# A Fourier-layer tower on one core: SBUF-to-SBUF seams, earlier group loads, and another order of squares in the mix

## The reference, cut to what matters

```python
for l in range(LAYERS):                                   # 4
    xf = rfft2(h)                                         # of every image and channel
    top = einsum('bixy,ioxy->boxy', xf[:, :, :16, :16], w1)
    bot = einsum('bixy,ioxy->boxy', xf[:, :, -16:, :16], w2)
    sc = irfft2(top and bot put into zeros)
    pw = einsum('bihw,oi->bohw', h, pw_w[l]) + pw_b[l]
    y = sc + pw
    y = (y - y.mean((0, 2, 3))) * rsqrt(y.var((0, 2, 3)) + EPS)   # over all images
    h = gelu(y * gamma[l] + beta[l])
```

## Time and profile before

| | |
|---|---|
| time before, median of 3 runs | 4336.68 us (4324.19 to 4337.49) |
| time of the profiled execution | 4346.47 us |
| its span, first to last instruction | 4344.7 us |
| mean granted TensorE clock | 0.880 of full speed |
| PE busy | 3227.5 us (74%) |
| DVE busy | 2415.4 us (56%) |
| ACT busy | 2244.2 us (52%) |
| POOL busy | 173.2 us (4%) |
| DMA moved | 798.68 MB, mean 184 GB/s |

### The profile page before, as it was taken

How to read it: one execution, slowest core, us unless ns; L and a number is a source line. 1 busy time by engine, 2 the same in 40 slices (tenths; PEclk the granted TensorE clock), 3 DMA queues, 4 the chain that set the end, 5 groups by cost and what they waited for, 6 DMA issues and landing times. The chain is left out here.

```text
span 4344.7 us, 119303 instructions
## 1 busy us (share of the span) xinstructions
PE 3227.5 (74%) x52804; PEld 1863.9 (43%) x52804; DVE 2415.4 (56%) x2474; ACT 2244.2 (52%) x2644; POOL 173.2 (4%) x249
## 2 busy tenths in 40 slices
PE   6758888885577677757577776755999996659777
PEld 4544444444444344435344343444444442543432
DVE  4545555554477677646577676744333332554556
ACT  3545566654466556546456555644666664222321
POOL 2013100000000000000000000000010102000000
PEclk8879999997799889878899888987999998669688
DMA  8857666667768878787678787887343331002042
GB/s 287 308 150 186 173 155 157 172 188 281 242 181 242 248 218 260 209 282 263 214 220 252 216 239 242 245 290 257 120 163 148 142 121 32 1 19 61 1 102 66
DMA packets 172143, 798.68 MB, mean 184 GB/s; under 512 B 31177, under 2 KB 37649, under 8 KB 122286
## 3 DMA queue, kind: packets, MB, share of 16 engines
q1 hardware_dynamic: 160796, 776.18, 58.8%
q0 software_dynamic: 7936, 13.65, 1.0%
q10 hardware_dynamic: 2898, 1.17, 0.1%
HBM read 448.68 MB, written 342.23 MB: 182 GB/s over the span
## 5 line engine op out<-in xcount | busy, mean ns | idle before, releaser
L828 PEld LDWEIGHTS bank<-fb,arena 64*64 64x64 f32 x16384 | 555.7, 196 | 540.1 <-issue 484.1
L828 PE MATMUL bank<-fb,arena 64*64 64x128 f32 x16384 | 619.7, 289 | 196.5 <-issue 140.7
L1045 ACT ACTIVATE arena<-bank 128x1024 f32<-128x1024 f32 x384 | 383.5, 1023 | 638.7 <-PE bank L973 423.7
L845 DVE TENSOR_TENSOR arena<-bank,arena 128x1024 f32<-128x1024 f32 x384 | 467.2, 1217 | 411.4 <-PE bank L828 408.8
L837 DVE STREAM_TRANSPOSE arena<-bank 128x1024 f32<-128x1024 f32 x256 | 318.8, 1245 | 535.7 <-PE bank L818 535.6
L1088 DVE STREAM_TRANSPOSE arena<-arena 128x1024 f32<-128x1024 f32 x384 | 458.3, 1212 | 134.2 <-ACT arena L1035 132.2
L818 PE MATMUL bank<-arena,ga 64*64 64x256 f32 x4096 | 308.8, 413 | 300.0 <-DMA arena<-spec_out 242.0
L973 PE MATMUL bank<-arena,wst 64*64 64x512 f32 x3072 | 414.7, 620 | 17.1 <-issue 11.1
L1052 ACT ACTIVATE arena<-arena 128x1024 f32<-128x1024 f32 x384 | 403.2, 1050 | 0.3
L1038 ACT ACTIVATE arena<-arena,shift,scale 128x1024 f32<-128x1024 f32 x256 | 316.3, 1236 | 129.2 <-DVE arena L845 127.0
L818 PEld LDWEIGHTS bank<-arena,ga 64*64 64x64 f32 x4096 | 167.3, 142 | 430.9 <-issue 359.3
(11 more groups left out here) (238 smaller groups left out, 3647.1 us busy)
## 6 DMA issues: line engine op xcount, KB each, us to landing
y_dram<-arena SPq DMA_DIRECT2D x384, 512.0 KB, 8.2
arena<-y_dram SPq DMA_DIRECT2D x96, 2048.0 KB
arena<-spec_in SPq DMA_DIRECT2D x32, 2048.0 KB, 10.0
spec_out<-arena SPq DMA_DIRECT2D x128, 512.0 KB, 8.2
arena<-in_w_modes SPq DMA_DIRECT2D x28, 2048.0 KB, 14.2
arena<-spec_out SPq DMA_DIRECT2D x112, 512.0 KB, 10.4
spec_in<-arena SPq DMA_DIRECT2D x96, 512.0 KB, 7.9
spec_in<-arena SPq DMA_DIRECT2D x8, 2048.0 KB, 12.5
```

Source lines behind the costliest of these rows:

```text
L828: mm = pe.matmul(hpx(bank[2 * s + i][CHAN[v], :])[:, :, j * S:(j + 1) * S], a2[p % 2][CHAN[i], :, v, 4 * T + j], hpx(fb2[CHAN[i], :]), sta ...
L845: dve.tensor_tensor(chunk(p, T), slot(s), chunk(p, T), ALU.add).then_inc(y_added, 1)
L1045: act.activation(chunk(p, T), slot(NEXT_SLOT[T]), ACT.Copy).then_inc(evicted, 1)
```

## The change

Of the fuse, three things change. Piece n+1 of the groups is issued at step n, where piece n was. The last group of new spectra goes straight from `xs` to the mix's buffer `s_sb` in four SBUF-to-SBUF copies of 64 KB for chunk 0 and four for chunk 1 (`load_last_group`); the seven earlier groups of these chunks are loaded from HBM ahead of it (`next_spectra`: for chunk 0 before the next layer's weights). The group is still stored to HBM too, for the chunks behind.

Of the seams: the barriers between the stages of the tower are gone, and named semaphores stand in their place. The part of the last mix chunk that pair 0 reads goes from `m_sb` to `grp[0]` in four SBUF-to-SBUF copies, ahead of the chunk's store. The last unit is turned before its sums are taken, and the batch norm's tiny chain is split up and runs between the fuse's first instructions. `m_sb` and `x2` move to other addresses, so that they don't lie on what the end of the fuse still reads.

Of the mix: `mix_done` is signalled for each half of a unit, ACT takes both squares ahead of the copies of the next product, and DVE takes its crosses in the order 0, 1 with no square behind them.

```diff
@@ sync_mix
+                for t in range(4):
+                    row = t % 2 * C + t // 2 * HB
+                    if c == NCH - 1:
+                        sp.dma_start(grp[0]...[row:row + HB, c],
+                                     m_sb[c % 2][t * HB:(t + 1) * HB, 0]...).then_inc(grp_loaded[0], 16)
                 for t in range(4):
                     sp.dma_start(spec_out[c, row:row + HB] ...
...
+                sp.wait_ge(spec_stored, l * (NG * 64) + 64)
+                sp.wait_ge(p_stored[0], l * (USES * 64))
+            load(2)
@@ tensor_mix.spectra
-                mm.then_inc(mix_done, 1)
+                    if swap == 1:
+                        mm.then_inc(mix_done, 1)
@@ scalar_mix
             for n in range(NU):
                 square(n, 0)
+                square(n, 1)
                 if n + 1 < NU:
                     for h in range(2):
                         copy_product(n + 1, h)
-                square(n, 1)
@@ vector_mix
-            for n in range(NU):
-                cross(n, 1)
+            for n in range(NU - 1):
                 cross(n, 0)
+                cross(n, 1)
                 turn(n)
...
+            turn(NU - 1)
+            cross(NU - 1, 1)
+            cross(NU - 1, 0)
@@ sync_fuse
+            def next_spectra(c, b, later):
+                sp.wait_ge(p_stored[b], l * (USES * 64) + USES * 64)
+                sp.wait_ge(squared, (l * NP + NP - later) * 4)
+                sp.wait_ge(spec_stored, l * (NG * 64) + (NG * 64))
+                load_spectra(sp, c, slice(0, NG - 1))
-            load_group(sp, l, 0, slice(NCH - 1, NCH))
+            load_piece(sp, l, 0)
             for n in range(NP + 2):
-                if n < NP:
-                    load_piece(sp, l, n)
+                if n + 1 < NP:
+                    load_piece(sp, l, n + 1)
                 if n > 1 and (n - 2) % Q == Q - 1:
+                    if n == NP + 1:
+                        sp.wait_ge(hdft_turned, (l * NP + NP) * 2)
+                        load_last_group(sp, 0, from_planes)
                     store_spectra((n - 2) // Q)
...
+                if n == NP - 1:
+                    next_spectra(0, 1, 2)
+            next_spectra(1, 3, 0)
+            sp.wait_ge(s_last_group, l * 128 + 192)
+            load_last_group(sp, 1, from_planes)
@@ tensor_fuse and tensor_last
+            pe.wait_ge(mixed_turned, (l * NU + NU - 1) * 2)
             rows_of(0, 0)
+            tensor_sums(pe, l)
             rows_of(0, 1)
@@ vector_fuse and vector_last
             turn_rows(dve, l, 0, 0, ROWS_SLOT[0])
+            vector_variance(dve, l)
             turn_rows(dve, l, 0, 1, ROWS_SLOT[1])
+            vector_scale(dve, l)
@@ each engine's program
-                phase_end(sp, l * 2 + 2)
                 sync_fuse(sp, l, False)
-                phase_end(sp, l * 2 + 3)
```

More of the change, by code:

```diff
@@ L546, in ahead @@
                         load_pair(sp, l, p)
-            for c in range(3):
-                load(c)
+            if first:
+                for c in range(2):
+                    load_spectra(sp, c, slice(0, NG - 1))
+                    if c > 0:
+                        sp.wait_ge(s_last_group, 64)
+                    load_last_group(sp, c, lambda c, v, ro: spec_in[c, ro * C + v * HB:ro * C + v * HB + HB, NG - 1])
+            else:
+                sp.wait_ge(spec_stored, l * (NG * 64) + 64)
+                sp.sem_inc(waited[sp.engine], 1)
+                sp.wait_ge(p_stored[0], l * (USES * 64))
+                sp.sem_inc(waited[sp.engine], 1)
+            load(2)
             for u in range(2):
@@ L632, in rotate @@
                 if c > 1:
-                    act.wait_ge(mix_done, (l * NCH + c) * 2 - 2)
-                act.activation(r_sb[c % 2][0:C], s_sb[c % 3][C:P], ACT.Copy, scale=-1.0).then_inc(imag_up, 1)
+                    act.wait_ge(mix_done, (l * NCH + c) * 4 - 4)
+                else:
+                    if c == 0 and not first:
+                        act.wait_ge(p_stored[2], l * (USES * 64))
+                        act.sem_inc(waited[act.engine], 1)
+                    act.activation(r_sb[c][0:C, 0:NG - 1], s_sb[c][C:P, 0:NG - 1], ACT.Copy, scale=-1.0)
+                    act.wait_ge(s_last_group, l * 128 + c * 64 + 64)
+                    act.sem_inc(waited[act.engine], 1)
+                gs = slice(NG - 1 if c < 2 else 0, NG)
+                act.activation(r_sb[c % 2][0:C, gs], s_sb[c % 3][C:P, gs], ACT.Copy, scale=-1.0).then_inc(imag_up, 1)
             def copy_product(n, h):
@@ L661, in scalar_mix @@
                         copy_product(n + 1, h)
-                square(n, 1)
                 if n % 2 == 0 and n // 2 + 1 < NCH:
                     rotate(n // 2 + 1)
-            act.wait_ge(bn_step, l * BN_STEPS + 7)
-            act.sem_inc(waited[act.engine], 1)
-            act.activation(bn[:, 14:15], bn[:, 13:14], ACT.Sqrt).then_inc(bn_root, 1)
+            scalar_root(act, l)
         BN_STEPS = 12
@@ L706, in turn @@
                     dve.sem_inc(waited[dve.engine], 1)
-                dve.wait_ge(s_squared, (l * NU + n) * 2 + 2)
+                if n == 2 and not first:
+                    dve.wait_ge(spec_stored, l * (NG * 64) + 64)
+                    dve.sem_inc(waited[dve.engine], 1)
+                if n == NU - 1:
+                    dve.wait_ge(mix_done, (l * NU + n) * 2 + 2)
                 dve.sem_inc(waited[dve.engine], 1)
@@ L1002, in h_dft @@
                 mm.then_inc(hdft_done, 1)
+            pe.wait_ge(mixed_turned, (l * NU + NU - 1) * 2)
+            pe.sem_inc(waited[pe.engine], 1)
             rows_of(0, 0)
+            tensor_sums(pe, l)
             rows_of(0, 1)
@@ L1032, in gelu @@
                 n = l * NP + p
+                if p == 0 and T == 0:
+                    act.wait_ge(bn_step, l * BN_STEPS + 12)
+                    act.sem_inc(waited[act.engine], 1)
                 if first:
@@ L1100, in h_turn @@
                 dve.wait_ge(hdft_done, l * NP + p + 1)
+                if p == 0:
+                    dve.wait_ge(mixed_stored[1], l * (NCH * 32) + NCH * 32)
+                    dve.sem_inc(waited[dve.engine], 1)
                 if q == 0:
@@ L1271, in gelu @@
             def gelu(p, T):
+                if p == 0 and T == 0:
+                    act.wait_ge(bn_step, L * BN_STEPS)
                 act.wait_ge(y_added, A + p * 4 + T + 1)
```

128 lines of the change are left out of this document (73 added, 55 removed).

## The result

The changed kernel takes 4127.7 us, the median of 4 runs (4116.2 to 4140.9), beside 4337.1 us for the kernel before on the same chip: a ratio of 0.952, 95% interval 0.948 to 0.956. Forecast were 4118 us (4040 to 4205). The profiled execution took 4140.9 us, span 4139.1, where the sum for it was 4127.5.

The account below looks back on a forecast made before the run. No engine is full: TensorE waits for group loads in the fuses and transfers in the seams. 112 + 47 + 33 + 28 - 1 = 219 us off the profiled 4346.5 gives 4127.5, or 4118 as median; range 4040 to 4205.

Parts of the forecast that it names:

- Group loads: Fuses: issuing group pieces one pair earlier removes most waits of TensorE's rows, saving 112 us (bounds 40 and 147).
- rival 1: Fuses: the pair load becomes as late as the piece was, giving 30 instead of 112: 4200 us, chance 0.14.
- the quarter "given back": Fuses: a queue that never drains gives back a quarter of the 147 us of group waits, leaving 112.
- Seam from fuse to mix: Last turn to first product: 10.6 instead of 26.2 us, saving 15.6, three times 47 us (bounds none and 69).
- rival 2: Both kinds of seam: copies land no earlier than the reload did and save nothing: 4198 us, chance 0.08.
- Seam from mix to fuse: Group 0 load to rows: 8.9 us less, four times 36, net 33 us (between 10 and 50).
- The mix's order: Mixes: DVE's turn no longer waits for ACT's second square, saving 28 us (bounds 0 and 56).
- 2.0 us less a chunk: Mixes: each rotating chunk loses 2.0 us; 7 chunks in 4 mixes make 56 us.
- I take half: Mixes: in places chunks come as the loads allow, so 28 of the order's 56 us are counted.
- The early half signal: Mixes: the first square starts 0.94 us earlier, keeping the next spectra within 0.1 us of their start.
- Rival 3: Fuses give nothing back (35 us) and the clock helps (28 us): 4055 us, chance 0.17.
- Rival 4: Fuses: SP's earlier piece waits for TensorE's rows and holds back a pair store and load: 4457 us, chance 0.03.

Follow-up runs that it names:

- u_groups: Changed kernel with the four pieces of a group issued as late as before, behind the pair's store and the next pair's load: 4239.5 us.
- b_groups: Kernel before with only the group pieces issued one pair earlier, seams and mix as before: 4220.6 us, ratio 0.970.
- u_copies: Changed kernel without SBUF-to-SBUF copies, both kinds of seam through HBM again, still without barriers: 4176.2 us.
- w_late: Changed kernel with the next layer's weights of chunks 1 and 2 issued behind the last-group copies: 4107.1 us.
- p_pairs: Changed kernel with the loads of pairs 0 and 1 issued behind the four copies of the mix's last chunk: 4092.4 us.
- u_mix: Changed kernel with the old order of squares, copies and crosses in the mix and one signal for a unit: 4167.2 us.
- bare_new: Changed kernel with most spectra and weight loads and stores cut to an eighth in the mixes of layers 1 to 3: 4051.5 us.

## Why the prediction was right

**Group loads (112 forecast, 111.4 measured).** The steps held: no wait of L886 for groups, the pair loads late once by 1.6 us (rival 1 falls), the DMA share above 0.8. u_groups brings 105 us back in the fuses, 112 between the medians. One sign did not come: the pairs of the middle fuses were to be even at 18 to 20 us, and they average 20.4 and 20.6, from 16.7 to 29.2. That is where the quarter "given back" went. In the two middle fuses 142.2 us of waits for groups are gone, but TensorE's "issue" time rose from 150.5 to 190.7 us, 40 us, 34 of them ahead of the second step of the forward transform (L999 before, L1086 changed); in the second fuse, before and changed:

```profile
PE bank L999 <- issue: 20.2, 8, 3.3
PE bank L1086 <- issue: 35.5, 14, 4.3
```

The quarter was argued from a queue that never drains, and the share did rise to 0.85; that the full queue makes these pauses isn't shown. Alone, b_groups gives 133 of the 147, a tenth back, at the same share. That 112 and 111.4 agree so closely is luck within the 6 us between two profiles.

**Seam from fuse to mix (47, measured 45.2).** 10.7 us from the copies' issue to the second mix against 10.6 worked out, and rival 2 falls: the copies land earlier than the reload, u_copies loses 27.8 us by it. The backlog in the sum (3.0 MB, 9.6 us) was the right thing to add up: w_late takes some out and wins 20.5.

**Seam from mix to fuse (33, measured 37.2).** "The pairs that pile up in front are what limits this part, not the barrier" is shown: p_pairs takes them out of the way for another 36 us. But 8.9 of the 37.2 are the mix's order, by u_mix, whose earlier last turn I had counted nowhere. What the term meant, copies instead of a barrier and a reload, is 28.3 (122.8 to 94.5), so it was 5 us too large, not 4 too small. The working fits the seams of layers 1 and 2, 8.7 and 8.6 us each; the last seam gave 3.8.

**The mix's order (28, measured about 30, from 25 to 39 by how it is taken).** The mixes alone show 16.4, and read so the term looks too large. u_mix shows 20.9 in the mixes, 8.9 in the seams. "2.0 us less a chunk" is borne out by undisturbed chunks at full clock (1.9), and "I take half" was right in size with traffic (7.5 a mix). The reason was half right. Some chunks do wait for their loads, but in the second mix the gain is taken back mostly elsewhere: TensorE waits 12.7 us less for DVE than in u_mix, and 7.1 us more for ACT's copies and in "issue" pauses. The early half signal was to keep the modes within 0.1 us of their time; the wait for the copies rose by 2.8 us in the 16 units of that mix, a little more than that.

**Others.** Rival 3 needed fuses without any loss and the clock on top: they gave 111, not 147. The granted clock did rise in the second fuse, 0.90 to 0.94, with no gain beyond the waits that I could separate. Rival 4 falls by SP's own waits in the second fuse: they are for the eviction of the pair to be stored (L1138) and for the turned spectra (L1200), none for TensorE's rows, so the pieces hold nothing back.

```profile
SPq L925 <- ACT arena L1138: 214.9, 21, 22.1
SPq L957 <- DVE arena L1200: 68.3, 7, 12.6
```

The profiled sum was 4127.5 and came out at 4140.9, 13.4 us more: the mixes' column gave 11.6 less than its term, the seams together 2.4 more and the fuses 0.6 less, and 4.6 us were lost outside the four stages; the 1 us put down for small costs goes the other way. The errors of single terms cancel in part, so the total is closer than the terms are.

## What to carry to other kernels

A transfer in the critical seam lasts as long as what was issued before it into the same queue: add those bytes up, at the seam's rate, before you shorten the transfer itself, and move loads with slack behind it. The sum is rough: for the two pair loads it gives 12.7 us (4.2 MB at 330 GB/s), and without them ahead the copies took 8.6 us less. At the seams into a fuse the order of four copies and two loads was worth 36.3 us; the copies themselves, against the way through HBM, 26.9. And measure an edit's worth by undoing it: the stage where it sits may show half, when part of the rest shows in the seam behind it, and one profile of each kernel may be off by 6 us.

## What was unexpected of the hardware

- TensorE paused up to 5.2 us for nothing that the profile names while the DMA engines stood at 0.91, and never above 1.4 us in the mix with their share at 0.32 (bare_new, 93 GB/s), with the same instructions. The granted clock was 0.90 in the first of these mixes and 0.97 in the second.
- Four copies of 64 KB from SBUF to SBUF took 9.3 us from issue to the rows with 1.75 MB issued just ahead of them, and 17.9 us with 4 MB more: 8.6 us for bytes that the rows didn't need.
- At the seams into a fuse the barriers cost next to nothing: u_copies, through HBM but without them, takes 28.1 us a seam, the kernel before 30.7, and of these 2.6 us the mix's order is 2.2. At the seams into a mix it takes 24.2 us, the kernel before 30.0; how much of these 5.8 is the barrier and how much the spectra loaded ahead, no run tells.
